# Grey picture of a vision layer: two DVE operations replaced by two scalings on ACT and two adding DMA transfers in DRAM

## The reference

```python
gray = jnp.einsum('bchw,c->bhw', x, (0.2989, 0.587, 0.114))[:, None]
edges = conv(gray, scharr)            # two 3x3 filters, zero padding
h = jnp.sqrt(jnp.square(edges)).sum(axis=1) / 2
h = h + attn(layernorm(h))            # mixes rows with the row before, k, v, r, wkv recurrence, Wo
h = h + ffn(layernorm(h))             # each row goes to its best expert of 8
```

## Time and profile before

| | |
|---|---|
| median of 3 runs | 1226.53 us (1224.15 to 1230.5) |
| profiled execution, its own time | 1227.5 us |
| its span, first to last instruction | 1225.7 us |
| PE busy | 1125.9 us, 92% |
| DVE busy | 1063.7 us, 87% |
| ACT busy | 813.7 us, 66% |
| Pool busy | 10.8 us, 1% |
| data moved | 140.07 MB, mean 114 GB/s |
| mean granted TensorE clock | 0.981 |

### The profile page before, as it was taken

How to read it: one execution, slowest core, us unless ns; L and a number is a source line. 1 busy time by engine, 2 the same in 40 slices (tenths; PEclk the granted TensorE clock), 3 DMA queues, 4 the chain that set the end, 5 groups by cost and what they waited for, 6 DMA issues and landing times.

```text
span 1225.7 us, 16385 instructions
## 1 busy us (share of the span) xinstructions
PE 1125.9 (92%) x5571; PEld 700.5 (57%) x5571; DVE 1063.7 (87%) x1860; ACT 813.7 (66%) x1323; POOL 10.8 (1%) x51
## 2 busy tenths in 40 slices
PE   1477799999999999999999999999999999999997
PEld 0222466665656566656665666566656665566666
DVE  2468899999999999999999999999999999998971
ACT  0245666876767667777677687676767777677652
POOL 3000000000000000000000000000000000000000
PEclk9778899999999999999999999999999999999999
DMA  5855344445553454455434545554344455521001
GB/s 171 195 124 121 90 125 124 101 121 133 141 131 112 118 129 94 127 132 140 128 107 117 131 94 131 132 140 124 105 120 124 100 136 132 140 65 44 18 18 35
DMA packets 145236, 140.07 MB, mean 114 GB/s; under 512 B 9440, under 2 KB 145206, under 8 KB 145206
## 3 DMA queue, kind: packets, MB, share of 16 engines
q1 hardware_dynamic: 145206, 139.69, 44.8%
HBM read 105.96 MB, written 33.69 MB: 114 GB/s over the span
## 4 chain that ended last, share of the span: by engine, by line
PE 74%; ACT 12%; issue 4%; DVE 4%; DMA 4%; SPq 1%; POOL 0%; ACTq 0%; POOLq 0%; DVEq 0%
PE bank L971 22%; PE bank L1110 13%; PE bank L1037 12%; PE bank L965 10%; PE bank L1014 10%; ACT hidden L830 4%; PE bank L1058 3%; ACT normed L845 3%; ACT normed_t L852 2%; ACT normed_hi L859 2%; DMA rows_in<-gray_dram 2%; PE bank L1088 1%; DVE normed_lo L637 1%; DMA gray_dram<-gray 1%; ACT gate L837 1%
## 5 line engine op out<-in xcount | busy, mean ns | idle before, releaser
L1110 PE MATMUL bank<-w_sb,hidden 128*128 128x256 f32 x1024 | 242.0, 383 | 1.0 <-ACT hidden L830 1.0
L1110 PEld LDWEIGHTS bank<-w_sb,hidden 128*128 128x128 f32 x1024 | 184.4, 190 | 35.3 <-issue 7.8
L762 ACT ACTIVATE v_sb<-bank 128x512 f32<-128x512 f32 x64 | 38.3, 598 | 201.6 <-PE bank L971 201.6
L965 PE MATMUL bank<-rows_in,conv_w 102*32 102x512 f32 x1024 | 132.5, 639 | 29.3 <-DMA rows_in<-gray_dram 29.3
L971 PE MATMUL bank<-mixed_r,w_r_t 128*128 128x512 f32 x256 | 122.6, 603 | 7.3 <-DVE mixed_r L536 7.3
L1014 PE MATMUL bank<-w_o_t,rwkv 128*128 128x256 f32 x512 | 124.3, 386 | 2.1 <-DVE rwkv L612 2.1
L1014 PEld LDWEIGHTS bank<-w_o_t,rwkv 128*128 128x128 f32 x512 | 94.6, 190 | 52.3 <-issue 40.0
L971 PE MATMUL bank<-mixed_v,w_v_t 128*128 128x512 f32 x256 | 123.6, 605 | 0.9 <-DVE resid L621 0.9
L971 PE MATMUL bank<-mixed_k,w_k_t 128*128 128x512 f32 x256 | 119.3, 609 | 0.8 <-DVE mixed_k L536 0.8
L1037 PE MATMUL bank<-normed_hi,w_hi 128*128 128x512 f32 x256 | 119.6, 467 | 0.0
L547 DVE TENSOR_TENSOR_SCAN max_state<-neg_exp_w,bank 128x256 f32<-128x256 f32 x128 | 80.6, 671 | 34.6 <-PE bank L971 34.6
(11 more groups left out here) (129 smaller groups left out, 1997.6 us busy)
## 6 DMA issues: line engine op xcount, KB each, us to landing
planes<-in_x_dram SPq DMA_DIRECT2D x64, 768.0 KB, 6.3
rows_in<-gray_dram SPq DMA_DIRECT2D x192, 256.0 KB
gray_dram<-gray SPq DMA_DIRECT2D x64, 258.0 KB, 2.9
out_dram<-resid SPq DMA_DIRECT2D x64, 256.0 KB, 2.2
rows_in<-gray_dram SPq DMA_DIRECT2D x128, 24.0 KB
hidden<-in_L_ffn_W_dram SPq DMA_DIRECT2D x2, 256.0 KB, 9.0
w_sb<-in_L_ffn_W_dram SPq DMA_DIRECT2D x1, 512.0 KB, 4.8
gate<-in_L_attn_Wk_dram SPq DMA_DIRECT2D x1, 256.0 KB, 5.8
```

Of the source, the lines that this page charges most:

```text
L762: act.activation(v_sb[:, 2 * ct:2 * ct + 2, :], pair_view(bank[BANK_V[ct]]), ACT.Copy).then_inc(s_v, 1)
L965: ins = pe.matmul(bank[BANK_EDGE[n]][ROW_TILE * q:ROW_TILE * (q + 1), :], conv_w[0:TAPS, c, :], rows, start=True, stop=True)
L1110: pe.matmul(ps, hidden[:, m, i, rows], w2_sb[:, m, :], start=(m == 0), stop=False)
```

## The change

The weighted sum is no longer made on DVE. SP loads only red and green into `planes[b]` (four transfers of 256 KB), and loads blue from the input straight into `gray_dram` (two transfers, DRAM to DRAM), once the convolution of the pair that used this buffer is over. ACT scales red and green in place by w0/w2 and w1/w2 (`scaled`), between `absolute(2)` and `copy_v(0)`. Pool, which had no work in the rounds before, issues two transfers that add red to `gray_dram` (`accum_op=ALU.add`), waits for them, and issues two that add green. SP waits for green and then loads `rows_in` as before. The tiny `tensor_tensor` on `pool_turn` carries Pool's waits. All of `gray_dram` is cleared at the start by one transfer of 1 MB and one of 8 KB, from zeros that Pool writes first of all into a part of `rows_in`; the old small border transfers and their wait for `s_built` go.

```diff
+        def gray_rows(buf, half):
+            return gray_dram[buf, :, 1 + half * P:1 + (half + 1) * P, 1:D + 1].rearrange("i p w -> p i w")
...
             def load_planes(j, c, buf):
+                first = j * (UNROLL * 2) + 2 * c
+                for plane in range(2):
+                    for half in range(HALF):
+                        src = x[bass.ds(first, 2), plane, half * P:(half + 1) * P, :]
+                        sp.dma_start(planes[buf][:, 2 * half:2 * half + 2, plane, :], src.rearrange("n p w -> p n w")
+                                     ).then_inc(planes_in[buf], 16)
+
+            def load_blue(j, c, buf):
                 for half in range(HALF):
-                    first = j * (UNROLL * 6) + 6 * c
-                    src = x_planes[bass.ds(first, 6), half * P:(half + 1) * P, :]
-                    sp.dma_start(planes[buf][:, 2 * half:2 * half + 2, :, :].rearrange("p i c w -> p (i c) w"),
-                                 src.rearrange("n p w -> p n w")).then_inc(planes_in[buf], 16)
+                    first = j * (UNROLL * 2) + 2 * c
+                    src = x[bass.ds(first, 2), 2, half * P:(half + 1) * P, :]
+                    sp.dma_start(gray_rows(buf, half), src.rearrange("n p w -> p n w")).then_inc(blue_in[buf], 16)
 
             load_planes(0, 0, 0)
+            sp.wait_ge(s_zeros, 1)
+            sp.dma_start(bass.AP(gray_dram.tensor, 0, [[8 * PITCH, P], [1, 8 * PITCH]]), zeros).then_inc(s_borders, 16)
...
-            sp.wait_ge(s_built, 1)
-            for k in range(2):
-                sp.dma_start(bass.AP(gray_dram.tensor, k * (T + 1) * PITCH, [[IMAGE, 4], [1, PITCH]]),
-                             zero_row[:, :]).then_inc(s_borders, 16)
-            sp.wait_ge(s_borders, 32)
-
             def step(at):
                 if at.has(LOAD) and not at.first():
-                    wait(sp, s_gray, at.count(LOAD, 1, 1, back=2))
+                    wait(sp, s_green, at.count(LOAD, 16 * HALF, 16 * HALF, back=2))
                     load_planes(at.j, at.u, at.buf(LOAD))
+                if at.has(LOAD) or at.has(GRAY):
+                    wait(sp, s_edge_ps, at.count(LOAD, 4, 4, back=2))
+                if at.first():
+                    sp.wait_ge(s_borders, 32)
+                if at.has(LOAD):
+                    load_blue(at.j, at.u, at.buf(LOAD))
                 if at.has(GRAY):
                     b = at.buf(GRAY)
-                    wait(sp, s_gray, at.count(GRAY, 1, 1))
-                    for half in range(HALF):
-                        if half == 1:
-                            wait(sp, s_edge_ps, at.count(GRAY, 4, 4, back=1))
-                        dst = gray_dram[b, :, 1 + half * P:1 + (half + 1) * P, :].rearrange("i p w -> p i w")
-                        sp.dma_start(dst, gray[:, 2 * half:2 * half + 2, :]).then_inc(gray_out[b], 16)
-                    wait(sp, gray_out[b], at.dma_count(GRAY, HALF))
+                    wait(sp, s_green, at.count(GRAY, 16 * HALF, 16 * HALF))
...
         @block.gpsimd
         def _(pool):
+            pool.memset(zeros, 0.0).then_inc(s_zeros, 1)
...
+            def step(at):
+                if not at.has(GRAY):
+                    return
+                b = at.buf(GRAY)
+                wait(pool, s_turn, at.count(GRAY, 2, 0))
+                wait(pool, blue_in[b], at.dma_count(GRAY, HALF))
+                wait(pool, s_scaled, at.count(GRAY, 2, 2))
+                pool.tensor_tensor(pool_turn[:, :], pool_turn[:, :], pool_turn[:, :], ALU.add).then_inc(s_turn, 1)
+                for half in range(HALF):
+                    pool.dma_start(gray_rows(b, half), planes[b][:, 2 * half:2 * half + 2, 0, :], accum_op=ALU.add
+                                   ).then_inc(s_red, 16)
+                wait(pool, s_turn, at.count(GRAY, 2, 1))
+                wait(pool, s_red, at.count(GRAY, 16 * HALF, 16 * HALF))
+                pool.tensor_tensor(pool_turn[:, :], pool_turn[:, :], pool_turn[:, :], ALU.add).then_inc(s_turn, 1)
+                for half in range(HALF):
+                    pool.dma_start(gray_rows(b, half), planes[b][:, 2 * half:2 * half + 2, 1, :], accum_op=ALU.add
+                                   ).then_inc(s_green, 16)
...
-            def gray_of(at):
-                if not at.has(GRAY):
-                    return
-                b = at.buf(GRAY)
-                wait(dve, planes_in[b], at.dma_count(GRAY, HALF))
-                wait(dve, gray_out[1 - b], at.dma_count(GRAY, HALF, back=1))
-                dve.scalar_tensor_tensor(out=gray[:, :, 1:D + 1], in0=planes[b][:, :, 0, :],
-                                         scalar=GRAY_WEIGHTS[0] / GRAY_WEIGHTS[2], in1=planes[b][:, :, 2, :],
-                                         op0=ALU.mult, op1=ALU.add).then_inc(s_red_blue, 1)
-                wait(dve, s_red_blue, at.count(GRAY, 1, 1))
-                dve.scalar_tensor_tensor(out=gray[:, :, 1:D + 1], in0=planes[b][:, :, 1, :],
-                                         scalar=GRAY_WEIGHTS[1] / GRAY_WEIGHTS[2], in1=gray[:, :, 1:D + 1],
-                                         op0=ALU.mult, op1=ALU.add).then_inc(s_gray, 1)
...
+            def scaled(c, at):
+                if not at.has(GRAY):
+                    return
+                b = at.buf(GRAY)
+                if c == 0:
+                    wait(act, planes_in[b], at.dma_count(GRAY, 2 * HALF))
+                act.activation(planes[b][:, :, c, :], planes[b][:, :, c, :], ACT.Copy,
+                               scale=GRAY_WEIGHTS[c] / GRAY_WEIGHTS[2]).then_inc(s_scaled, 1)
```

More of the change, by code:

```diff
@@ L95, in vision_layer @@
     X_DMAS = 10
-    x_planes = x.rearrange("n c h w -> (n c) h w")
     gray_dram = nc.dram_tensor("gray_dram", [2, 2, T + 2, PITCH], F32).ap()
@@ L105, in sem @@
             return ctx.enter_context(nc.semaphore(name))
-        planes = [sb(f"planes{i}", [P, NB, NCOL, D]) for i in range(2)]
-        gray = sb("gray", [P, NB, PITCH])
+        planes = [sb(f"planes{i}", [P, NB, 2, D]) for i in range(2)]
+        pool_turn = sb("pool_turn", [P, 1])
         rows_in = sb("rows_in", [P, TILES, 2, D])
-        zero_row = sb("zero_row", [4, PITCH])
         edge = [sb(f"edge{i}", [P, NB, D]) for i in range(4)]
@@ L174, in vision_layer @@
         w1_scaled = resid[0][:, :, :].rearrange("p (a b) d -> p a (b d)", a=CH)
+        zeros = rows_in[:, :, :, :].rearrange("p t i w -> p (t i w)")[:, 0:8 * PITCH]
         w1_raw = hidden[:, 0:2, :, :].rearrange("p a b c -> p a (b c)")
@@ L187, in vision_layer @@
         planes_in = [sem(f"planes_in{i}") for i in range(2)]
+        s_zeros = sem("zeros")
         s_params_in, s_scharr_dj_in, s_borders = sem("params_in"), sem("scharr_dj_in"), sem("borders")
@@ L193, in vision_layer @@
         s_dve_setup, s_act_setup, s_pe_setup = sem("dve_setup"), sem("act_setup"), sem("pe_setup")
-        gray_out = [sem(f"gray_out{i}") for i in range(2)]
+        blue_in = [sem(f"blue_in{i}") for i in range(2)]
+        s_red, s_green, s_turn = sem("red"), sem("green"), sem("turn")
         s_rows_loaded = sem("rows_loaded")
         stored = [sem(f"stored{i}") for i in range(4)]
-        s_red_blue, s_gray = sem("red_blue"), sem("gray_done")
+        s_scaled = sem("scaled")
         s_edge_ps, s_abs, s_edge = sem("edge_ps"), sem("abs"), sem("edge_done")
@@ L249, in load_planes @@
             def load_planes(j, c, buf):
+                first = j * (UNROLL * 2) + 2 * c
[5 more added lines that the diff above has]
+            def load_blue(j, c, buf):
                 for half in range(HALF):
-                    first = j * (UNROLL * 6) + 6 * c
-                    src = x_planes[bass.ds(first, 6), half * P:(half + 1) * P, :]
-                    sp.dma_start(planes[buf][:, 2 * half:2 * half + 2, :, :].rearrange("p i c w -> p (i c) w"),
-                                 src.rearrange("n p w -> p n w")).then_inc(planes_in[buf], 16)
+                    first = j * (UNROLL * 2) + 2 * c
+                    src = x[bass.ds(first, 2), 2, half * P:(half + 1) * P, :]
+                    sp.dma_start(gray_rows(buf, half), src.rearrange("n p w -> p n w")).then_inc(blue_in[buf], 16)
             load_planes(0, 0, 0)
+            sp.wait_ge(s_zeros, 1)
+            sp.dma_start(bass.AP(gray_dram.tensor, 0, [[8 * PITCH, P], [1, 8 * PITCH]]), zeros).then_inc(s_borders, 16)
+            sp.dma_start(bass.AP(gray_dram.tensor, P * 8 * PITCH, [[PITCH, 8], [1, PITCH]]), zeros[0:8, 0:PITCH]
+                         ).then_inc(s_borders, 16)
             for dj in range(3):
@@ L364, in _ @@
                                ).then_inc(s_cleared, 1)
-            pool.memset(zero_row[:, :], 0.0)
-            pool.memset(gray[:, :, 0:1], 0.0)
-            pool.memset(gray[:, :, D + 1:D + 2], 0.0)
+            pool.memset(pool_turn[:, :], 0.0)
             pool.memset(normed_t[:, :, 0:1], 0.0)
@@ L379, in _ @@
             pool.memset(route[:, :, :], 0.0).then_inc(s_built, 1)
+            def step(at):
```

(5 more changed lines are left out.)

## The result

The changed kernel takes **1249.14 us** (median of 4 runs, 1247.01 to 1250.29), the kernel before beside it on the same chip 1225.45: a ratio of 1.0184 [1.015, 1.0217] (95% interval), slower by 23.7 us by the medians. Forecast were 1246 us and +19.7.

A forecast was written before the change was run, and what follows sets the result against it. PE was taken to bound the loop, with the gray picture's way critical only in the ramp. DVE, ACT and loop terms were booked as 0; 1226.5 + 19.7 for pairs 0 to 2 gave 1246 us, range 1229 to 1300.

The forecast's parts named there:

- DVE's removed work: Two gray operations on DVE, 2.44 us a round, booked as 0 because PE ends the wait before `residual(1)`.
- The scalings lie in ACT's hole: On ACT ahead of `copy_v(0)`: two scalings, 2.1 us a round, fit the 4.72 us hole, leaving 2.6; booked as 0.
- The loop hides the additions: In the loop, rows are loaded at 549.8 and the convolution stands at 556.4: 6.6 us spare, round still 35.15 us.
- The limit at which the loop waits: In the loop, the round lengthens only where 3.45 + 2.1 + 2R + 10 is over 35.15 us: R over 9.8 us.
- R: Time of one addition to the gray picture: two transfers from Pool's queue, Pool's small operation and the semaphore; taken as 6.5 us.
- rival 2: Additions so slow that the loop waits: from R = 9.8 some 27 rounds each get 2(R - 9.8) longer; chance 0.15.
- Start-up: Before pair 0: Pool's clearing 1.9 us more, ACT's exponential at 18.2 instead of 16.20, planes ready at about 22.0 us.
- The ramp: Pairs 0 to 2 wait for the longer way of the gray picture: convolutions at 47.9, 82.2 and 116.6, +19.7 us.
- 6R - 19.3: General form of the loss over pairs 0 to 2 at the start; +19.7 us at the R taken.
- Pair 3: End of the ramp: its old round of 36.7 us exceeds 34.4, so the loss stops; adds 2R - 15.2 where R is over 7.6.
- The two-port rule: Pool's queue cannot write DMA descriptors while DVE runs in a two-port mode; expected to leave the loop nearly alone.

The follow-up runs named there:

- e6: The kernel before, with DVE leaving out the second gray operation (green) in the loop's rounds: 1226.14 us, ratio 1.0003.
- e1: The changed kernel, with the gray pictures of pairs 0 to 2 made on DVE and written by SP as before: 1226.52 us, ratio 1.0006.
- e3: The changed kernel with a third addition per pair, red added again behind green: 1448.57 us, ratio 1.1835.
- e4: The changed kernel with the adding transfers turned into plain writes from Pool's queue: 1234.17 us, ratio 1.0077.
- e5: The changed kernel, clearing only the borders of the scratch by five small transfers instead of all of it: 1249.13 us, ratio 1.0192.
- e8: The kernel before, with pair 1's gray ahead of DVE's expert set-up and pair 2's planes loaded behind pair 1's row loads: 1219.52 us, ratio 0.9954.
- e10: e3 plus five matmuls on constants per loop round, ahead of the first convolution where PE would wait: 1418.41 us, ratio 1.1573.

## Why the prediction was right

- **DVE's removed work is worth nothing.** Right: its waits for PE grew from 0.77 to 1.22 + 1.86 = 3.1 us (3.2 forecast), and e6 shows it alone for one of the two operations.
- **The scalings lie in ACT's hole.** Right: 1.99 us, 2.83 left (2.6 forecast).
- **The loop hides the additions.** Right: round 35.16 us, some 6 us spare (6.6), and e1's round of 35.15 us shows 29 pairs for nothing. The limit at which the loop waits was placed at R = 9.8, and e3, with 22 us of additions in place of 19.6 at that limit, waits; but the price beyond the limit, in rival 2, was far too low. At R = 11 it would have given 1345 us, and e3, with as much in the way, took 1449. Two terms of its condition were short: 3.45 us to `absolute(2)`'s end holds only while PE's clock is up (5.8 in e3's round shown), and the row loads took 11.7 us in e3's mean and not 10. With 11.7 the limit would lie near R = 9.0.
- **R = 6.5 us.** Somewhat short, 7.4 measured. The sum from the plain write and the reading back had the right parts, but the write from Pool's queue takes 4.7 us with Pool's operation and the semaphore, rather than the 3.5 of SP's plus 0.5, and the adding 2.7 rather than 2.5. The Trainium skill, "DMA: Bandwidth & Descriptors", "Anatomy of one DMA", by whose figures R would be an estimated 3.2 us, is off by more than half, and by a third for e4's plain write.
- **Start-up.** Oversized. `exp_w` stands at 16.57, 0.4 us later and not 2, and the planes are scaled at 20.1, not at 22.0. The 1 MB of zeros delays nothing (e5), and Pool's clearing, 1.82 us long, no more than these 0.4 us. This made up for R in pair 0: the first row load was due at 35.0 and stood at 35.16, with 20.1 + 15.1 in place of 22.0 + 13.0.
- **The ramp.** The mechanism is right: three convolutions late, one behind the other. They were forecast at 47.9, 82.2 and 116.6 and measured at 48.0, 83.8 and 121.0. In general 6R - 19.3 with R = 7.4 gives 25.1; less 1.9 for the start-up, 23.2, for the 24.0 seen at pair 2. Pair 3 gives 1.1 back: its round is 35.54 us, ruled by the gray picture by then (PE waits 0.19 us), where before it took 36.7.

That 1246 came so near is thus partly luck: R was short by 6 x 0.9 = 5.4 us, and the start-up's 1.9 us and the 1.1 us of pair 3 went the other way.

## What to carry to other kernels

Follow the transfer chain once in the steady loop and once in the ramp: a chain that is hidden by half a round of slack can be the critical path for the first pairs, and there every microsecond of it counts once per pair until the pipeline is full. Freeing an engine that is 87% busy brought nothing, since it was waiting for PE already behind the freed place, while a shorter start of the kernel before (e8) brought 6 us with the loop untouched. Price a rival "the loop will wait" with the granted clock in mind: where PE's wait closes a loop with its own work, the slow clock behind the wait makes the next round late as well (1.7 us a round in e3). And read the length of a transfer where it stands ahead of a waiting engine, not where it is hidden: the row loads were taken at 10 us from a round in which nobody waits for them, and took 11.7 in e3, where PE does.

## What the runs showed of the hardware

- Two adding transfers of 256 KB from Pool's queue to DRAM, in rows of 1 KB: some 7.4 us in the ramp and 7.1 in the loop, including Pool's small operation and the semaphore, against 4.7 us in the ramp for plain ones (e4). Pool needs 1.2 us to issue one adding transfer, 0.72 for a plain one.
- With DVE 79% busy over the span, Pool's issuing time for two adding transfers hardly moved (2.40 to 2.44 us, 2.61 for the first pair); once there was a gap of 0.96 us ahead of it, the cause of which is open. The two-port rule that the prediction weighed did not show in these times. Pool's small `tensor_tensor`, though, took 1.98 us in place of 0.18 beside a DVE scan (e3).
- In e3's loop, behind waits of PE of 3.8 to 4.8 us the 24 convolution matmuls took 4.4 to 5.4 us instead of 2.7, with the granted clock at 0.5 in the round shown; behind the four shorter waits, 2.05 to 2.37 us, they took 2.78 (twice), 3.75 and 4.48. With the wait filled by matmuls (e10) they took 2.78, and the clock stayed at 1.00.
